# Reordering the opening of a two-layer kernel on one core: batch 1's choice first, batch 2's ranks ahead of the first tile, and products of ones in TensorE's waits

## The chip, the cores and the metric

The kernel runs on one core of one Trainium2 chip. The core has TensorE (PE, with its weight loads PEld), VectorE (DVE), ScalarE (ACT), GpSimd (POOL) and SyncE (SP), which work through five separate lists of instructions and wait for each other on semaphores only. The metric is the device time of one execution in microseconds, the median of several.

## The reference

The input x has 8 batches of 512 rows of 128 numbers. Two residual layers are computed in float32:

```python
x = x + _layernorm(_L0_attn_ref(_layernorm(x, axis=-1), W_in, b_in, W_out, b_out, decay, mix), axis=-1)
x = x + _layernorm(_L0_ffn_ref(_layernorm(x, axis=-1), gate_kernel, w0, w1, wo), axis=-1)
```

The first layer mixes each row with the row before it (`mix * x + (1 - mix) * shifted`), multiplies by `W_in`, adds a bias, takes relu, runs a decaying sum down the sequence (`state = state * decay + h_t`) and multiplies by `W_out`. The second is a mixture of experts: each row is multiplied by a gate of 8 columns, the two largest logits choose two of 8 experts, and each chosen expert computes

```python
layer_1 = _gmm(sorted_hidden, w0, onehot)
layer_2 = _gmm(sorted_hidden, w1, onehot)
intermediate = jax.nn.silu(layer_1) * layer_2
layer_3 = _gmm(intermediate, wo, onehot)
```

with inner width 512. The two results of a row are summed with softmax weights.

## The kernel before, in words

**Two halves.** The 4096 rows make 8192 pairs of row and expert. The first layer goes batch by batch (512 rows each, four blocks of 128). The second goes tile by tile: 71 tiles of 128 pairs that belong to one expert. Between the two lies a table in DRAM, `expert_rows`, with a region for each expert. After a batch is chosen, its rows are written there by 8 indirect DMAs that GpSimd issues (`send_row`, L394). A tile is read back by one plain DMA that SyncE issues (`load_tile`, L312).

**What a batch does, in order.** `start1` and `offset1` (DVE) give the first norm, `normalise1` (ACT) applies it, `turn1` (PE, L1298) turns the four blocks, `shift` (ACT) and `mix_rows` (DVE, L757) mix the rows, `times_w_in` (PE, L1306) multiplies, `relu` (ACT), `scan` (DVE, L765) is the decaying sum, `times_w_out` (PE, L1313 and L1317) multiplies again. `start2` and `residual` (DVE, L771, L780) norm the result and add it to x. `start3`, `offset3` (DVE), `normalise3` (ACT, L524), `turn2` (PE, L1326), `turned` (ACT, L531) and `times_gate` (PE, L1333) lead to the gate's logits. `top` and `choose` (DVE, L812 to L839) pick the two experts. `ranks` (PE, L1340 to L1349) counts how many earlier rows went to each expert, and `put` (DVE, L846 to L866) makes the places in the table from it. `send_row` waits for those places. From batch 2 on, the roots of the second norm are taken by GpSimd (`late_power`, L382 and L385).

**The table of tiles.** `full_tiles` to `use_tiles` (DVE, L880 to L938) find out which expert and which rows each of the next 8 tiles has. Phase 1 (tiles 0 to 7) needs batches 0 and 1. SyncE waits for that table and then for all rows of both batches to have landed (L325) before it loads tile 0.

**Weights.** w0 and w1 are each split in two parts. ACT rounds a piece (`round_w`, L537, 8 pieces). The remainders are subtracted by GpSimd for w0 and by DVE for w1 (`split_rest`, L256, 8 half pieces).

**Order.** Each engine's list is written out by hand: an opening, and then a loop over slots, one tile to a slot, in which pieces of the later batches (`a_slot`) are interleaved with the tiles. In slot t PE turns tile t (L1376), multiplies tile t-1 by w0 and w1 (L1381 to L1383, six products), turns back tile t-2 (L1416) and multiplies tile t-3 by wo (L1432). `x_hi` (ACT, L570) and `x_lo` (DVE, L1099) split a turned tile before it is multiplied. In slot 1 PE turns batch 4 (`turn1(4)`, L1298), for which batch 3's `residual` must be done, because both use one bank of PSUM. In the kernel before, DVE's `put(2)` and PE's `ranks(2)` and `times_w_out(3)` stand in slot 0, behind tile 0.

## Time and profile before

| what | value |
|---|---|
| median of 3 runs | 347.58 us (345.55 to 349.6) |
| the profiled execution | 350.95 us, span 349.2 us |
| mean granted clock of TensorE | 0.858 |
| busy: PE, PEld | 262.5 us (75%), 220.8 us (63%) |
| busy: DVE, ACT, POOL | 199.7 us (57%), 179.4 us (51%), 180.1 us (52%) |
| first tile on PE | 64.72 us |
| last matmul | before 320 us |

Busy time is an average over three stages that have different limits: the opening up to the first tile at 64.72 us, the tiles, and the last norm after some 320 us. The granted clock is the share of full speed (2.4 GHz) that TensorE had; 0.50 is 1.2 GHz. The span is the time between the first and the last record of the profiled execution, and its own time is 1.75 us longer.

### The profile page before, as it was taken

Reading aid. Unit: us, or ns where it says so; the run is one execution under the profiler, and the core shown is the slowest. Engines: PE = TensorE matmul, PEld = TensorE weight load, DVE = VectorE, ACT = ScalarE, POOL = GpSimd, SP = SyncE. Lnnn points to the kernel's source line nnn. Section 1 sums busy time; section 2 is a strip of 40 time slices with the busy share of each in tenths; the row PEclk is TensorE's granted clock in tenths of the full one; section 3 lists DMA queues with packets and bytes.
Section 4 is the critical chain, followed back from the end, with each engine's and each line's share of the span. In section 5 each row is a group of like instructions: output and inputs, shape, how many; then the busy total and the mean of one; then the engine's idle time right before and its main releaser. Section 6 shows DMA issues by size and latency. Waiting matters only on the chain.

```text
span 349.2 us, 6768 instructions
## 1 busy us (share of the span) xinstructions
PE 262.5 (75%) x1615; PEld 220.8 (63%) x1615; DVE 199.7 (57%) x896; ACT 179.4 (51%) x436; POOL 180.1 (52%) x199
## 2 busy tenths in 40 slices
PE   1645515579997999699969969969999999995000
PEld 0323513468785888588858858848888888885000
DVE  4787969564662495348347625633334455459763
ACT  3475635345654566354545544524655565554362
POOL 6065567155465656545754764465333333335673
PEclk9975555589999899789989998998999999999555
DMA  6999111211221131013112211331233100190225
GB/s 160 225 362 281 41 38 55 52 33 41 60 57 46 41 76 48 30 52 81 41 35 64 57 47 42 83 92 55 69 85 79 42 23 23 31 401 29 90 60 150
DMA packets 27971, 29.48 MB, mean 84 GB/s; under 512 B 4538, under 2 KB 21148, under 8 KB 27936
## 3 DMA queue, kind: packets, MB, share of 16 engines
q1 hardware_dynamic: 22672, 20.00, 20.2%
q0 software_dynamic: 4544, 8.93, 8.0%
q8 instruction: 16, 0.26, 0.3%
q10 hardware_dynamic: 720, 0.13, 0.2%
q14 instruction: 19, 0.16, 0.2%
HBM read 17.49 MB, written 12.01 MB: 84 GB/s over the span
## 4 chain that ended last, share of the span: by engine, by line
PE 60%; DVE 15%; ACT 8%; another core or an unknown queue 6%; POOL 4%; issue 4%; DMA 2%; SPq 0%; ACTq 0%; DVEq 0%; POOLq 0%
PE bank L1432 14%; PE bank L1381 9%; PE bank L1383 9%; PE bank L1382 8%; PE bank L1416 8%; PE bank L1376 3%; POOL expert_rows L394 2%; PE bank L1317 2%; PE bank L1333 2%; ACT sb_w_raw L593 2%; DVE sb_rs L1171 2%; PE bank L1326 2%; ACT sb_row L524 1%; PE bank L1306 1%
## 5 line engine op out<-in xcount | busy, mean ns | idle before, releaser
L405 POOL DMA_INDIRECT pair_rows<-sb_y_rows,sb_y_pair x71 | 70.4, 991 | 99.3 <-ACT sb_y_rows L587 75.2
L394 POOL DMA_INDIRECT expert_rows<-sb_row,sb_place x64 | 65.1, 1016 | 32.0 <-issue 18.0
L1106 DVE TENSOR_TENSOR sb_w_raw<-bank,sb_w_raw 128x512 f32<-128x512 f32 x71 | 49.0, 690 | 51.9 <-PE bank L1383 33.7
L1432 PE MATMUL bank<-sb_w_raw,sb_gatedT 128*128 x568 | 76.4, 279 | 0.0
L1432 PEld LDWEIGHTS bank<-sb_w_raw,sb_gatedT 128*128 128x128 f32 x568 | 70.6, 196 | 0.1
L1381 PE MATMUL bank<-sb_w_parts,sb_x_hi 128*128 x142 | 65.2, 459 | 3.5 <-ACT sb_w_raw L575 1.9
L580 ACT ACTIVATE sb_gatedT<-bank 128x512 f32<-128x512 f32 x71 | 42.5, 599 | 45.3 <-PE bank L1416 32.0
L1099 DVE TENSOR_TENSOR sb_x_lo<-bank,sb_x_hi 128x128 fp32r<-128x128 f32 x71 | 20.4, 288 | 66.9 <-ACT sb_x_hi L570 60.6
L1383 PE MATMUL bank<-sb_w_parts,sb_x_hi 128*128 x142 | 58.5, 412 | 0.0
L1382 PE MATMUL bank<-sb_w_parts,sb_x_lo 128*128 x142 | 58.1, 409 | 0.0
L575 ACT ACTIVATE sb_w_raw<-bank 128x512 f32<-128x512 f32 x71 | 42.7, 601 | 18.4 <-PE bank L1383 14.3
L570 ACT ACTIVATE sb_x_hi<-bank 128x128 fp32r<-128x128 f32 x71 | 19.7, 277 | 58.2 <-PE bank L1376 35.7
L1416 PE MATMUL bank<-sb_ident,sb_w_raw 128*128 128x128 f32 x284 | 44.2, 280 | 0.4 <-issue 0.4
L1416 PEld LDWEIGHTS bank<-sb_ident,sb_w_raw 128*128 128x128 f32 x284 | 35.5, 144 | 9.9 <-issue 2.6
L1381 PEld LDWEIGHTS bank<-sb_w_parts,sb_x_hi 128*128 128x128 f32 x142 | 28.2, 199 | 10.3 <-issue 6.9
L1383 PEld LDWEIGHTS bank<-sb_w_parts,sb_x_hi 128*128 128x128 f32 x142 | 28.1, 198 | 7.0
L1382 PEld LDWEIGHTS bank<-sb_w_parts,sb_x_lo 128*128 128x128 f32 x142 | 28.4, 200 | 3.2
L1376 PE MATMUL bank<-sb_ident,sb_taken_rows 128*128 128x128 f32 x71 | 20.4, 287 | 4.6 <-DMA sb_taken_rows<-expert_rows 4.0
L587 ACT ACTIVATE sb_y_rows<-bank 128x128 f32<-128x128 f32 x71 | 19.5, 274 | 1.0 <-PE bank L1432 0.9
L1306 PE MATMUL bank<-sb_early,sb_w_inT 128*128 128x512 f32 x16 | 11.4, 803 | 10.2 <-DVE sb_early L757 10.2
L1326 PE MATMUL bank<-sb_ident,sb_row 128*128 128x128 f32 x32 | 7.5, 378 | 14.4 <-ACT sb_row L524 14.3
L256 POOL TENSOR_TENSOR sb_w_parts<-sb_w_raw,sb_w_parts 128x512 fp32r<-128x512 f32 x8 | 9.9, 1271 | 15.4 <-ACT sb_w_parts L537 15.4
(162 smaller groups left out, 353.4 us busy)
## 6 DMA issues: line engine op xcount, KB each, us to landing
sb_taken_rows<-expert_rows SPq DMA_DIRECT2D x71, 65.0 KB
sb_w_raw<-in_L_ffn_w SPq DMA_DIRECT2D x2, 2048.0 KB, 15.1
sb_w_raw<-pair_rows SPq DMA_DIRECT2D x2, 1024.0 KB, 7.8
out_dram<-sb_x SPq DMA_DIRECT2D x3, 512.0 KB, 3.2
pair_rows<-sb_y_rows,sb_y_pair POOLq DMA_INDIRECT x71
sb_x<-in_L_attn_x SPq DMA_DIRECT2D x4, 256.0 KB, 5.5
expert_rows<-sb_row,sb_place POOLq DMA_INDIRECT x64
sb_w_raw<-pair_rows SPq DMA_DIRECT2D x2, 512.0 KB, 3.4
```

The source lines that it names most:

```text
L394: pool.indirect_dma_start(expert_rows[:, :], bass.IndirectOffsetOnAxis(ap=place[b % ROWS][:, k, j:j + 1], axis=0), row[b % ROWS][:, j, :], ...
L405: pool.indirect_dma_start(pair_rows[:, :], bass.IndirectOffsetOnAxis(ap=y_pair[group % 2][:, t % PAIRS:t % PAIRS + 1], axis=0), y_rows[slo ...
L575: act.activation(silu[t % 2][:], p_l1[:], ACT.Silu).then_inc(c["silu"], 1)
L580: act.activation(gatedT[t % 2][:], p_gatedT[:], ACT.Copy).then_inc(c["gatedT"], 1)
L1099: dve.tensor_tensor(x_lo[t % 2][:], p_xeT[:, 0:P], x_hi[t % 2][:].bitcast(F32), ALU.subtract).then_inc(c["x_lo"], 1)
L1106: dve.tensor_tensor(gated[t % 2][:], p_l2[:], silu[t % 2][:], ALU.mult).then_inc(c["gated"], 1)
L1376: pe.transpose(p_xeT[:, 0:P], taken_rows[:, t % RING, 0:D], ident[:]).then_inc(c["xeT_ps"], 1)
L1381: pe.matmul(to, x_hi, w_hi, start=True, stop=False)
L1382: pe.matmul(to, x_lo, w_hi, start=False, stop=False)
L1383: return pe.matmul(to, x_hi, w_lo, start=False, stop=True)
L1416: last = pe.transpose(p_gatedT[:, n * P:(n + 1) * P], gated[t % 2][:, n * P:(n + 1) * P], ident[:])
L1432: last = pe.matmul(p_y[t % 2][:, 0:D], gatedT[t % 2][:, n * P:(n + 1) * P], wo.rearrange("p o d -> p (o d)"), start=(n == 0), stop=(n == F ...
```

## The change

It touches the opening of four engines and slot 0 of the loop.

- DVE: `offset1(3)`, `top(1)`, `choose(1)` and `put(1)` move ahead of `rest_mean_var` and `start2(2)`. `put(2)` moves out of slot 0, in front of the loop. Five of the eight half pieces of `split_rest` come last. The last steps of the table of phase 1 stand behind `top(2)` and `choose(2)`.
- ACT: `round_w(4)` and `round_w(5)` move ahead of `normalise3(1)`; `relu(3)` ahead of `root(3, 2)`; `rest_root` and `turned(2)` change places with others.
- PE: `times_gate(1)` moves ahead of `times_w_out(2)`; `ranks(2)` and `times_w_out(3)` move out of slot 0, in front of tile 0. A new function `fill(n)` issues n products of ones with ones, 128x128 by 128x512 in bf16, into the bank `p_l1` that nothing else uses before tile 0. There are 60 such products in 12 places.

```diff
@@ ACT, opening
             root(3, 1, mv3, sd3)
+            round_w(4)
+            round_w(5)
             normalise3(1, 0, G)
-            round_w(4)
             turned(1)
             root(1, 3, mv1, sd1)
-            round_w(5)
-            rest_root()
+            round_w(6)
+            normalise1(3, 0, G)
+            round_w(7)
+            shift(3)
             root(2, 2, mv2, sd2)
-            round_w(6)
-            round_w(7)
-            normalise1(3, 0, G)
-            shift(3)
+            relu(3)
             root(3, 2, mv3, sd3)
             normalise3(2, 0, G)
+            rest_root()
+            turned(2)
             act.activation(unused[:], eps[:], ACT.Silu)
-            relu(3)
-            turned(2)
             normalise1(4, 0, G)
@@ DVE, slot 0 and opening
                 if s == 0 and part == 0:
-                    if k == 0:
-                        put(2)
                     if table:
                         full_tiles(p)
...
             rest_sums(8, 16)
-            rest_mean_var()
-            start2(2)
+            offset1(3)
             top(1)
             choose(1)
-            offset1(3)
             put(1)
+            start2(2)
+            mix_rows(3)
+            residual(2)
+            start3(2)
             split_rest(0, 1)
-            residual(2)
+            offset3(2)
+            rest_mean_var()
             split_rest(1, 3)
-            start3(2)
-            mix_rows(3)
-            split_rest(3, 4)
-            offset3(2)
+            scan(3)
+            rest_offset()
             full_tiles(1)
             expert_ends(1)
             experts_past(1)
             experts_of_tiles(1)
+            top(2)
+            choose(2)
             rows_skipped(1)
             rows_of_tiles(1)
             use_tiles(1)
-            split_rest(4, 6)
-            scan(3)
-            split_rest(6, 8)
-            rest_offset()
-            top(2)
-            choose(2)
+            put(2)
+            split_rest(3, 8)
@@ PE
+            def fill(n):
+
+                for _ in range(n):
+                    pe.matmul(p_l1[:], ones_b[:],
+                              ones_b[:, None, :].broadcast_to([P, G, P]), start=True, stop=True)
...
                 if part == 0:
-                    if k == 0 and s == 0:
-                        ranks(2)
-                        times_w_out(3)
...
             times_w_in(1)
+            fill(2)
             turn1(2)
+            fill(3)
             times_w_out(1)
+            fill(10)
             times_w_in(2)
             turn2(0)
+            fill(2)
             times_gate(0)
+            fill(7)
             ranks(0)
+            fill(5)
             turn2(1)
+            fill(2)
+            times_gate(1)
             times_w_out(2)
-            times_gate(1)
+            fill(1)
             ranks(1)
             turn1(3)
+            fill(6)
             times_w_in(3)
+            fill(8)
             turn2(2)
+            fill(2)
             times_gate(2)
+            times_w_out(3)
+            ranks(2)
+            fill(12)
```

VectorE from batch 3's first norm to batch 1's choice, before (`sb_rest_mv` belongs to the norms of batches 4 to 7, L771 to `start2(2)`, L812 to L819 to `top(1)`):

```order
L737 BN_STATS sb_rest_stats<-sb_x 128x6 x8
L744 BN_AGGR sb_rest_mv<-sb_rest_stats 128x2 x16
L771 BN_STATS sb_stats_0<-bank 128x6 x4
L707 BN_AGGR sb_mv_0<-sb_stats_0 128x2 x4
L812 MAX sb_top_1<-bank 128x8 x4
L816 MAX_INDEX sb_choice_1<-sb_top_1,bank 128x8 x4
```

and the same place in the changed kernel (L714 and L720 are `offset1(3)`):

```order
L737 BN_STATS sb_rest_stats<-sb_x 128x6 x8
L714 RECIPROCAL sb_rs_1<-sb_sd_1 128x4
L720 SCALAR_TENSOR_TENSOR sb_nm_1<-sb_mv_1,sb_rs_1 128x4
L812 MAX sb_top_1<-bank 128x8 x4
L816 MAX_INDEX sb_choice_1<-sb_top_1,bank 128x8 x4
```

Two groups of norms no longer stand in front of the choice.

VectorE at the end of the opening, in the changed kernel, from the last step of `choose(2)` over the table (L917 to L938) and `put(2)` (L846 to L866) to tile 0's `x_lo` (L1097 there):

```order
L839 TENSOR_REDUCE sb_taken<-sb_taken 128x8
L917 TENSOR_REDUCE sb_skipped<-sb_past_skip 128x8
L919 TENSOR_SCALAR sb_tile_chunk_i<-sb_tile_expert 128x8
L926 SCALAR_TENSOR_TENSOR sb_tile_row_i<-sb_tile_f,sb_used,sb_skipped 128x8
L932 TENSOR_SCALAR sb_clipped<-sb_ends 128x9
L935 TENSOR_TENSOR sb_take<-sb_clipped 128x8
L938 TENSOR_TENSOR sb_used<-sb_used,sb_take 128x8
L846 TENSOR_TENSOR sb_rank_f<-bank,sb_region_f 128x32
L856 TENSOR_SCALAR sb_count_i<-bank 128x8
L861 TENSOR_TENSOR sb_place_0<-sb_onehot,sb_rank_f 128x32 x2
L866 TENSOR_REDUCE sb_place<-sb_place_0 128x8
L256 TENSOR_TENSOR sb_w_parts<-sb_w_raw,sb_w_parts 128x4x128 x5
```

Before, tile 0's `x_lo` stood directly behind L839; the four rows L846 to L866 followed it, and the table and the five half pieces had been done earlier.

TensorE around tile 0 (the first L1376), before:

```order
L1326 MATMUL bank<-sb_ident,sb_row 128x128 x4
L1333 MATMUL bank<-sb_gate,sb_early 128x8 x4
L1376 MATMUL bank<-sb_ident,sb_taken_rows 128x128
L1340 MATMUL bank<-sb_taken,sb_ones_b 128x8
L1342 MATMUL bank<-sb_taken,sb_before_b 128x32
L1346 MATMUL bank<-sb_taken,sb_ones_b 128x24
L1346 MATMUL bank<-sb_taken,sb_ones_b 128x16
L1346 MATMUL bank<-sb_taken,sb_ones_b 128x8
L1349 MATMUL bank<-sb_taken,sb_ones_b 128x32
L1313 MATMUL bank<-sb_b_parts,sb_ones_b 128x512
L1317 MATMUL bank<-sb_w_outT,sb_early 128x128 x4
```

and in the changed kernel (L1294 are the products of ones, L1316 and L1320 `times_w_out(3)`, L1343 to L1352 `ranks(2)`):

```order
L1294 MATMUL bank<-sb_ones_b 128x512 x2
L1336 MATMUL bank<-sb_gate,sb_early 128x8 x4
L1316 MATMUL bank<-sb_b_parts,sb_ones_b 128x512
L1320 MATMUL bank<-sb_w_outT,sb_early 128x128 x4
L1343 MATMUL bank<-sb_taken,sb_ones_b 128x8
L1345 MATMUL bank<-sb_taken,sb_before_b 128x32
L1349 MATMUL bank<-sb_taken,sb_ones_b 128x24
L1349 MATMUL bank<-sb_taken,sb_ones_b 128x16
L1349 MATMUL bank<-sb_taken,sb_ones_b 128x8
L1352 MATMUL bank<-sb_taken,sb_ones_b 128x32
L1294 MATMUL bank<-sb_ones_b 128x512 x12
L1376 MATMUL bank<-sb_ident,sb_taken_rows 128x128
```

Batch 2's ranks and batch 3's product now stand in front of tile 0, and twelve products of ones between them and it.

## Rows read from the trace of the kernel before

**Rows 1.** Windows: busy us (instructions) per engine, TensorE's granted clock, DMA share, GB/s
```profile
core 0: us, PE busy (x) PEld busy (x) DVE busy (x) ACT busy (x) POOL busy (x), PEclk, DMA share, GB/s
20.00:25.00 5.00, 2.02 (x9) 1.70 (x9) 4.82 (x17) 3.50 (x5) 4.05 (x4) 0.66 1.05 376
...
60.00:65.00 5.00, 0.99 (x6) 0.83 (x6) 2.96 (x22) 1.65 (x4) 0.39 (x1) 0.50 0.11 27
```

**Rows 2.** Chain of waits, 59 to 86 us: start us, us, what
```profile
59.43 2.29 DMA expert_rows<-sb_row,sb_place
...
65.35 0.42 PE bank L1313
...
72.51 0.23 PE bank L1381
...
76.09 0.34 PE bank L1381
...
78.03 0.89 PE bank L1432 x8
...
84.89 0.23 PE bank L1313
```

**Rows 3.** Timeline, POOL: start us, us, engine, line, op [idle before it and its releaser]
```profile
36.96 1.09 POOL L394 DMA_INDIRECT expert_rows<-sb_row,sb_place  x1 [4.60 <-DVE sb_place L866]
...
49.38 0.96 POOL L394 DMA_INDIRECT expert_rows<-sb_row,sb_place  x1 [2.47 <-DVE sb_place L866]
50.65 1.88 POOL L394 DMA_INDIRECT expert_rows<-sb_row,sb_place  x1 [0.30 <-issue]
```

**Rows 4.** Timeline, DVE, opening
```profile
32.71 0.39 DVE L812 MAX8 sb_top<-bank 128x8 f32<-128x8 f32 x4 [1.24 <-PE bank L1333]
...
35.83 0.22 DVE L866 TENSOR_REDUCE sb_place<-sb_place 128x8 int32<-128x64 f32 x1
...
44.80 0.17 DVE L825 CAST sb_choice_f<-sb_choice 128x8 f32<-128x8 uint32 x1 [1.15 <-DVE sb_choice L816]
45.51 0.23 DVE L828 TENSOR_TENSOR sb_onehot<-sb_expert_f,sb_choice_f 128x64 bf16<-128x64 f32 x1 [0.54 <-DVE sb_choice_f L825]
...
48.35 0.22 DVE L866 TENSOR_REDUCE sb_place<-sb_place 128x8 int32<-128x64 f32 x1 [1.14 <-DVE sb_place L861]
...
50.40 1.29 DVE L256 TENSOR_TENSOR sb_w_parts<-sb_w_raw,sb_w_parts 128x512 fp32r<-128x512 f32 x2
...
57.01 1.29 DVE L256 TENSOR_TENSOR sb_w_parts<-sb_w_raw,sb_w_parts 128x512 fp32r<-128x512 f32 x2
...
62.98 0.22 DVE L839 TENSOR_REDUCE sb_taken<-sb_taken 128x8 bf16<-128x40 bf16 x1
65.53 0.29 DVE L1099 TENSOR_TENSOR sb_x_lo<-bank,sb_x_hi 128x128 fp32r<-128x128 f32 x1 [2.33 <-ACT sb_x_hi L570]
65.74 0.18 DVE L846 TENSOR_TENSOR sb_rank_f<-bank,sb_region_f 128x32 f32<-128x32 f32 x1
...
66.42 0.16 DVE L880 TENSOR_SCALAR sb_tiles_i<-sb_count_i 128x8 int32<-128x8 int32 x1
...
67.63 0.89 DVE L771 BATCH_NORM_STATS2 sb_stats<-bank 128x6 f32<-128x128 f32 x4 [0.64 <-PE bank L1317]
```

**Rows 5.** Timeline, PE, opening
```profile
26.77 2.07 PE L1306 MATMUL bank<-sb_early,sb_w_inT 128*128 128x512 f32 x2 [3.53 <-DVE sb_early L757]
...
30.69 1.87 PE L1333 MATMUL bank<-sb_gate,sb_early 128*128 128x8 f32 x8 [0.69 <-ACT sb_early L531]
34.90 0.19 PE L1340 MATMUL bank<-sb_taken,sb_ones_b 128*128 128x8 bf16 x1 [2.34 <-DVE sb_taken L839]
...
64.72 0.47 PE L1376 MATMUL bank<-sb_ident,sb_taken_rows 128*128 128x128 f32 x1 [4.01 <-DMA sb_taken_rows<-expert_rows]
...
71.77 0.63 PE L1298 MATMUL bank<-sb_ident,sb_early 128*128 128x128 f32 x4 [1.87 <-DVE sb_x L780]
```

**Rows 6.** Timeline, ACT: `normalise3(1)`
```profile
35.16 1.65 ACT L524 ACTIVATE sb_row<-sb_x,sb_nm,sb_rs 128x128 f32<-128x128 f32 x4 [3.66 <-DVE sb_nm L720]
```

## The prediction

> **What bounds the opening now.** I read the page first, then the windows, the chain of waits, and the timelines of POOL, DVE and PE up to 72 us. The windows show TensorE losing its clock between 20 and 25 us (granted 0.66), and at half speed, 1.2 GHz, in the last one before the tiles, with 0.99 us of work in 5 [rows 1]. That alone costs nothing where PE waits for others. The chain says who it waits for: the last row send of batch 1 is issued at 59.43 us and landed 2.29 us later [rows 2], and tile 0 is turned at 64.72 us, 3.0 us behind that landing, after 4.01 us of idle time [rows 5]. GpSimd issues the sixteen sends from 36.96 us. Batch 0's end at 46.91 us (49.38 less the idle 2.47), and then GpSimd sits until batch 1's places come [rows 3]. So the opening is bounded by GpSimd's sixteen sends and by VectorE, which delivers both sets of places.
>
> VectorE is nearly as tight. From the end of `put(0)` at 36.05 us to the end of `choose(2)` at 63.20 us lie 27.15 us of its list, of which 2.83 us are three waits for its own results (1.15, 0.54, 1.14 us) in batch 1's choice and places, the stretch under batch 0's sends and just behind them [rows 4]. Then it idles 2.33 us until tile 0 is turned.
>
> Behind tile 0 the point to watch is `turn1(4)` at 71.77 us, before which PE idles 1.87 us for batch 3's residual [rows 5]. It hangs on `sums2(3)`, which DVE starts at 67.63 us after 0.64 us of idle time for `times_w_out(3)` [rows 4]. From there to `turn1(4)` are 4.14 us through DVE and POOL that the change does not touch.
>
> **The change, part by part.**
>
> *Ones before `ranks(0)`.* In front of `top(0)` DVE idles 1.24 us for the gate's products, which take 1.87 us at half clock [rows 4, 5]. If the ones hold the clock, nearly all of that idle time goes; I leave 0.09 us, so **1.15 us** are won, and `put(0)` ends at 34.9 us, the first send starts at 35.8 us. The bounds: 1.24 us, and a loss if the ones are late themselves (rival D). The price of one product of ones is that of the nearest row, the bias product over 512 columns in bf16: 0.23 us in a dense stream at full clock, 0.42 us at half [rows 2]. Ten take 2.3 us in a gap of 3.53, seven 1.6 us in a gap of 2.34 [rows 5]; at full clock they cost nothing.
>
> *Batch 1's choice first.* `put(1)` now comes right after batch 3's first norm, some 8 us after `put(0)`, stalls included, so at about 43 to 45 us, before batch 0's sends are out (35.8 + 9.95 = 45.75). GpSimd's wait of 2.47 us goes. The last send starts at 35.8 + 9.95 + 0.30 + 10.05 = 56.1 us (batch 0's eight, a gap, batch 1's from first to last start [rows 3, 2]), has landed at 58.4 us, and tile 0 can be turned at 61.4 us, `x_lo(0)` 0.81 us later at 62.2 us. By the sends alone the gain there is 65.53 - 62.2 = 3.3 us.
>
> *VectorE's sum.* Its list up to `x_lo(0)` holds the same work as before and `put(2)`, 0.68 us (65.74 to 66.42) [rows 4]: 34.9 + 27.15 + 0.68 = **62.7 us**, if it stalls as often as before. That is 0.5 us later than the sends allow, so DVE sets the time. The table of phase 1 comes before five half pieces (5 x 0.645 = 3.2 us, from the pairs of 1.29), `put(2)` and some 0.45 us, at 58.4 us, together with the landing. The five half pieces used to stand before a wait of 2.33 us, where a late DVE cost nothing; now they stand on the path.
>
> *Slot 0.* Before, `sums2(3)` began 2.10 us after `x_lo(0)` (65.53 to 67.63): `put(2)` 0.68 and 0.64 of waiting are now gone, and 0.78 us remain. So `sums2(3)` starts at 62.7 + 0.8 = 63.5 us, **4.1 us** earlier than 67.63, and `turn1(4)` at 67.7 us.
>
> *ACT.* `round_w(4)` and `(5)` move into the 3.66 us that it waited in front of `normalise3(1)` [rows 6] and take about 2 us there: nothing. If that cover were gone, `normalise3(1)` would be late by as much, but batch 1's gate has slack until DVE asks for it some 4 us later.
>
> *The last twelve ones.* They follow `ranks(2)`, at about 58 us by the sums above, and end near 61 us at full clock, just in front of tile 0: nothing. At half clock they end at 63.1 us and hold tile 0 back by 1.7 us, `x_lo(0)` by 1.2 us.
>
> *After `turn1(4)`.* Before, tile 1's products there ran partly at half clock: 3.58 us from its first product (72.51) to tile 2's (76.09), less 0.21 for a turn, where tile 2's took 1.94 us (76.09 to 78.03) [rows 2]. Up to 1.4 us lie in that. But PE will idle there again for batch 3's residual, some 2.5 us, longer than the 1.87 us of before, so I take nothing and keep 1.4 us as the bound above; below, a clock lower still for one more tile costs 1.4 us.
>
> *The tiles.* After 72 us PE is the engine that is busy throughout, and its list, like those of the others, is unchanged. The sends of batch 2 are interleaved with the tiles and move with them. A shift of the start is a shift of the end.
>
> The sum is 4.1 us. The profiled execution took 350.95 us, so it would take 346.9. It lies 3.4 us above the median of the three runs, which themselves spread over 4 us; against the median of 347.58 us the forecast is **343.5 us**.
>
> **A rule against this change.** One send took 1.88 us instead of 0.96 [rows 3]; it started at 50.65 us, while DVE subtracted half pieces, with two inputs from SBUF (50.40, 1.29 us) [rows 4]. The stalls of DVE's small steps came in the stretch of the sends as well. In the changed kernel sends run without a break from 35.8 to 57 us, and batch 2's choice moves into their last part. I give this as rival C, from the rows, and its extreme as E. The Trainium skill, GPSIMD Engine Reference, section 1 (Specifications), says that GpSimd shares its SBUF interfaces with VectorE and contends with instructions that have two SBUF inputs or run in a two-port mode. By that rule the stretched send and the stalls are one thing, and more overlap means more of both.
>
> **The rivals.**
>
> A. The forecast: as many stalls as before, clock held. Chance 0.50, its own range 341.8 to 345.5 us.
>
> B. *More.* The stalls do not recur, and a send isn't stretched (0.9 us less). Then the sends bound: `x_lo(0)` at 61.3, `sums2(3)` at 62.1, a gain of 5.5 us; with the full clock after `turn1(4)` 6.9. Time 340.7 to 342.1 us. For it: `choose(2)` and the table ran before almost without a stall. Against it: batch 1's choice lies under sends as it did. Chance 0.15.
>
> C. *GpSimd's sends stall batch 2's choice too.* Another 2.83 us in DVE's list, which has no slack left: a gain of 1.3 us, 346.3 us. Chance 0.18.
>
> D. *The ones don't hold the clock.* Then they cost 0.42 us each and stand ahead of work that is waited for. Ten take 4.2 us from 23.24 to 27.4, where 26.77 was the start of the next product; seven more end at 36.2 us, where `ranks(0)` started at 34.90. Everything is 2.45 us later than in A, and the last twelve end at 65.6 us: `x_lo(0)` 66.4, `sums2(3)` 67.2, a gain of 0.4 us, 347.2 us. Against it: two stretches of ones are the densest work that PE gets there. Chance 0.09.
>
> E. *Slower.* The same mechanism as C, at DVE's end of the opening: batch 1's choice, batch 2's choice, the table's fourteen dependent steps and `put(2)` with the half pieces each stall 2.83 us under sends. Each stall counts in full, since the 2.33 us of idle time in front of `x_lo(0)` are gone: 4 x 2.83 - 2.83 = 8.5 us against 4.1, so 352.0 us. It decides from 6.9 us of stalls on, and is slower by 1% from 10.4. For it: three stalls came in one batch. Against it: the table's steps ran before under batch 1's sends almost freely, between 54 and 57 us. Chance 0.08.
>
> **How the numbers follow.** A difference of 1%, 3.5 us, is about what a measurement of this kernel can tell from none. The forecast lies only 0.6 us beyond it. B and three quarters of A are faster by more, 0.52; a quarter of A, C and D are within, 0.40; E is slower, 0.08. The range of 340.5 to 347.5 us takes in A, B, C and D, and leaves out E and the outer ends.
>
> **What would show it.** Right: granted clock near 1 between 25 and 60 us, DVE without the wait in front of `top(0)`, sixteen sends of GpSimd with no wait longer than 0.5 us between them, tile 0 turned at about 61.5 us, and `turn1(4)` at about 67.7 us. C or E: waits of DVE for its own results in `choose(2)` or the table, and `x_lo(0)` at 65 us or later with tile 0 turned before. D: granted clock 0.50 and ones ending after the work behind them was ready. The forecast would be wrong in kind if the tiles behind 72 us do not keep the distance that the opening won.

## The result, and the profile after

The changed kernel takes 352.8 us (median of 4 runs, 351.38 to 353.7). The kernel before, beside it, takes 348.09 us (4 runs, 345.55 to 349.6). The ratio is 1.0134, 95% interval [1.0085, 1.0184]: **slower by 1.3%**, where 343.5 us and a gain of 4.1 us were forecast. The profiled execution of the changed kernel took 352.79 us (span 351.1, granted clock 0.904), that of the kernel before 350.95 us. Some executions of a kernel take over 1.5% longer than its fastest (the profiled one of the kernel before, 350.95 against 345.55 us, is such a one), and every ratio in this document leaves these out, so that a ratio and two medians may differ.

The sends come first, since they were the aim. GpSimd's own list is the same in both kernels; what moves its sends is when their places come. GpSimd's timeline of the changed kernel (start, duration, instruction, [idle time before it and its releaser]):

```profile
37.47 1.09 POOL L394 DMA_INDIRECT expert_rows<-sb_row,sb_place  x1 [5.08 <-DVE sb_place L866]
...
47.75 0.96 POOL L394 DMA_INDIRECT expert_rows<-sb_row,sb_place  x1 [0.30 <-issue]
...
56.60 0.96 POOL L394 DMA_INDIRECT expert_rows<-sb_row,sb_place  x1 [0.30 <-issue]
70.11 1.22 POOL L394 DMA_INDIRECT expert_rows<-sb_row,sb_place  x1 [12.54 <-DVE sb_place L866]
```

They did what the change was to do: sixteen sends with 0.30 us between them, the last one starting at 56.60 us instead of near 59 [rows 2]. Tile 0 no longer waits for them. It waits for TensorE, whose timeline is:

```profile
30.72 1.87 PE L1336 MATMUL bank<-sb_gate,sb_early 128*128 128x8 f32 x8
32.45 3.15 PE L1294 MATMUL bank<-sb_ones_b 128*128 128x512 bf16 x7
...
43.38 0.64 PE L1301 MATMUL bank<-sb_ident,sb_early 128*128 128x128 f32 x4
43.85 1.46 PE L1294 MATMUL bank<-sb_ones_b 128*128 128x512 bf16 x6
48.99 2.08 PE L1309 MATMUL bank<-sb_early,sb_w_inT 128*128 128x512 f32 x2 [3.69 <-DVE sb_early L757]
50.86 3.62 PE L1294 MATMUL bank<-sb_ones_b 128*128 128x512 bf16 x8
61.79 1.11 PE L1329 MATMUL bank<-sb_ident,sb_row 128*128 128x128 f32 x4 [7.30 <-ACT sb_row L524]
...
67.98 3.16 PE L1294 MATMUL bank<-sb_ones_b 128*128 128x512 bf16 x12
70.97 0.31 PE L1376 MATMUL bank<-sb_ident,sb_taken_rows 128*128 128x128 f32 x1
...
77.08 0.63 PE L1301 MATMUL bank<-sb_ident,sb_early 128*128 128x128 f32 x4 [2.67 <-DVE sb_x L780]
```

Tile 0 (L1376) is turned at 70.97 us, 6.25 us later than before [rows 5]. In front of it PE stood idle for 7.30 us before `turn2(2)` (L1329), waiting for ACT's `normalise3(2)`. ACT's timeline shows why that was late:

```profile
47.47 0.69 ACT L508 ACTIVATE sb_early<-bank,sb_one_minus_mix 128x511 f32<-128x511 f32 x1 [4.05 <-remote]
...
58.77 0.69 ACT L513 ACTIVATE sb_early<-bank,sb_b_in 128x512 f32<-128x512 f32 x1 [10.43 <-issue]
...
60.09 1.65 ACT L524 ACTIVATE sb_row<-sb_x,sb_nm,sb_rs 128x128 f32<-128x128 f32 x4 [0.34 <-issue]
...
71.32 0.28 ACT L570 ACTIVATE sb_x_hi<-bank 128x128 fp32r<-128x128 f32 x1 [4.73 <-PE bank L1376]
```

These two waits are the finding of the case. `shift(3)` (L508) reads what PE's `turn1(3)` wrote. PE's record of that ends at 43.38 + 0.64 = 44.02 us, but ACT starts at 47.47. `relu(3)` (L513) reads the product that ended at 48.99 + 2.08 = 51.07 us, but ACT starts at 58.77, 7.7 us later, having done nothing for 10.43. PE has only the eight ones left to do, and they end at 50.86 + 3.62 = 54.48 us, 4.3 us before `relu(3)` starts. By the records no engine is at work on anything that ACT needs. Nor is ACT short of instructions: the queues that carry them move nothing between 43.5 and 78 us of this trace. The profile names no releaser. "Remote" means that an update of the awaited semaphore is recorded just before the start, but long after the recorded end of the work; "issue" means that no such update is found in the records. The chain of waits (start, duration, what) has the same two pieces:

```profile
42.48 0.95 ACT sb_w_parts L537
43.42 4.03 another core or an unknown queue
47.45 0.02 issue
47.47 0.69 ACT sb_early L508
48.16 0.18 ACT sb_sd L481
48.34 10.43 issue
58.77 0.69 ACT sb_early L513
```

I call such a stretch a **late signal**: the work waited for is recorded as done, the waiting engine is free, and it starts microseconds later. It is a name for what is seen, not yet a cause: the profile models the ends of PE's products, so a product may also have ended later than its record says. For `shift(3)` the update of the semaphore is on record at 47.45 us, 3.4 us behind that end. The Trainium skill, Perfetto Trace Analysis, section Per-engine timelines, draws the propagation of a semaphore update as a stage of its own behind an instruction's recorded end. That agrees with what is seen, but the page gives it no such length, and 7.7 us is this trace's number.

VectorE's timeline shows the consequence:

```profile
32.75 0.39 DVE L812 MAX8 sb_top<-bank 128x8 f32<-128x8 f32 x4 [1.23 <-PE bank L1336]
...
35.79 0.19 DVE L846 TENSOR_TENSOR sb_rank_f<-bank,sb_region_f 128x32 f32<-128x32 f32 x1 [0.64 <-PE bank L1352]
...
44.62 0.19 DVE L846 TENSOR_TENSOR sb_rank_f<-bank,sb_region_f 128x32 f32<-128x32 f32 x1 [1.47 <-PE bank L1352]
...
48.19 0.75 DVE L757 SCALAR_TENSOR_TENSOR sb_early<-bank,sb_mix,sb_early 128x512 f32<-128x512 f32 x1 [1.47 <-ACT sb_early L508]
...
59.68 0.18 DVE L714 RECIPROCAL sb_rs<-sb_sd 128x4 f32<-128x4 f32 x1 [7.37 <-ACT sb_sd L481]
...
65.61 0.39 DVE L812 MAX8 sb_top<-bank 128x8 f32<-128x8 f32 x4 [0.47 <-PE bank L1336]
...
72.22 0.28 DVE L1097 TENSOR_TENSOR sb_x_lo<-bank,sb_x_hi 128x128 fp32r<-128x128 f32 x1
...
72.94 0.89 DVE L771 BATCH_NORM_STATS2 sb_stats<-bank 128x6 f32<-128x128 f32 x4
```

`offset3(2)` (L714) needs a root that stands on ACT behind `relu(3)`, and 7.37 us pass. Behind it stand batch 2's choice, the table of tiles 0 to 7 and `put(2)`.

Last the windows (engines' busy time, then granted clock, DMA share, GB/s):

```profile
20.00:25.00 5.00, 4.86 (x26) 2.81 (x24) 4.82 (x17) 3.49 (x5) 4.04 (x4) 0.90 1.06 377
25.00:30.00 5.00, 2.20 (x7) 1.29 (x8) 4.56 (x26) 3.15 (x8) 3.50 (x4) 0.79 1.05 289
30.00:35.00 5.00, 5.00 (x18) 2.62 (x16) 3.52 (x28) 3.35 (x6) 2.40 (x2) 0.50 1.01 279
...
55.00:60.00 5.00, 0.00 (x0) 0.00 (x0) 0.29 (x3) 0.97 (x3) 1.95 (x3) 0.84 0.12 40
```

The ones raised the clock before 30 us, from 0.66 in the window from 20 to 25 us [rows 1] to 0.90, and lost it where it was wanted: 0.50 from 30 to 35 us, with `times_gate(0)` and `ranks(0)` in it. From 55 to 60 us PE does nothing at all.

### The profile page after: what moved, and what is told of

It reads as the page before. It is cut to its first block, busy times and chain, and to the rows that moved or that the text cites. A ratio compares the mean times of both kernels' runs of the same rounds, so it can differ in the third digit from the quotient of the medians.

```text
span 351.1 us, 6888 instructions
## 1 busy us (share of the span) xinstructions
PE 272.6 (78%) x1675; PEld 219.7 (63%) x1675; DVE 199.1 (57%) x896; ACT 178.6 (51%) x436; POOL 180.0 (51%) x199
## 4 chain that ended last, share of the span: by engine, by line
PE 55%; DVE 12%; ACT 11%; issue 8%; another core or an unknown queue 7%; POOL 4%; DMA 2%; SPq 0%; ACTq 0%; DVEq 0%; POOLq 0%
PE bank L1432 13%; PE bank L1383 8%; PE bank L1381 8%; PE bank L1382 8%; PE bank L1416 7%; ACT sb_row L524 2%; PE bank L1336 2%; PE bank L1376 2%; PE bank L1294 2%; PE bank L1329 2%; ACT sb_w_raw L593 2%; DVE sb_rs L1169 2%; ACT sb_early L498 1%; PE bank L1320 1%
## 5 line engine op out<-in xcount | busy, mean ns | idle before, releaser
L394 POOL DMA_INDIRECT expert_rows<-sb_row,sb_place x64 | 64.8, 1013 | 36.0 <-issue 18.3
L1432 PE MATMUL bank<-sb_w_raw,sb_gatedT 128*128 x568 | 75.0, 275 | 0.0
L1432 PEld LDWEIGHTS bank<-sb_w_raw,sb_gatedT 128*128 128x128 f32 x568 | 69.0, 192 | 0.1
L1381 PE MATMUL bank<-sb_w_parts,sb_x_hi 128*128 x142 | 63.8, 449 | 1.5 <-DVE sb_w_raw L1104 0.6
L1097 DVE TENSOR_TENSOR sb_x_lo<-bank,sb_x_hi 128x128 fp32r<-128x128 f32 x71 | 20.5, 288 | 66.6 <-ACT sb_x_hi L570 52.2
L1383 PE MATMUL bank<-sb_w_parts,sb_x_hi 128*128 x142 | 56.8, 400 | 0.0
L1382 PE MATMUL bank<-sb_w_parts,sb_x_lo 128*128 x142 | 56.5, 398 | 0.0
L1416 PE MATMUL bank<-sb_ident,sb_w_raw 128*128 128x128 f32 x284 | 43.0, 274 | 0.7 <-issue 0.7
L1416 PEld LDWEIGHTS bank<-sb_ident,sb_w_raw 128*128 128x128 f32 x284 | 34.4, 141 | 10.5 <-issue 3.4
L1381 PEld LDWEIGHTS bank<-sb_w_parts,sb_x_hi 128*128 128x128 f32 x142 | 27.5, 194 | 8.8 <-issue 5.8
L1383 PEld LDWEIGHTS bank<-sb_w_parts,sb_x_hi 128*128 128x128 f32 x142 | 27.1, 191 | 6.6
L1382 PEld LDWEIGHTS bank<-sb_w_parts,sb_x_lo 128*128 128x128 f32 x142 | 27.5, 194 | 3.0
L1376 PE MATMUL bank<-sb_ident,sb_taken_rows 128*128 128x128 f32 x71 | 20.1, 282 | 4.7 <-DVE sb_x_lo L1097 2.6
L1329 PE MATMUL bank<-sb_ident,sb_row 128*128 128x128 f32 x32 | 7.2, 366 | 18.7 <-ACT sb_row L524 16.6
L1294 PE MATMUL bank<-sb_ones_b 128*128 128x512 bf16 x60 | 21.2, 501 | 0.0
L1329 PEld LDWEIGHTS bank<-sb_ident,sb_row 128*128 128x128 f32 x32 | 4.9, 187 | 21.9 <-ACT sb_row L524 19.1
```

Of the source, the lines that this page charges most:

```text
L394: pool.indirect_dma_start(expert_rows[:, :], bass.IndirectOffsetOnAxis(ap=place[b % ROWS][:, k, j:j + 1], axis=0), row[b % ROWS][:, j, :], ...
L1294: pe.matmul(p_l1[:], ones_b[:], ones_b[:, None, :].broadcast_to([P, G, P]), start=True, stop=True)
L1376: pe.transpose(p_xeT[:, 0:P], taken_rows[:, t % RING, 0:D], ident[:]).then_inc(c["xeT_ps"], 1)
L1381: pe.matmul(to, x_hi, w_hi, start=True, stop=False)
L1382: pe.matmul(to, x_lo, w_hi, start=False, stop=False)
L1383: return pe.matmul(to, x_hi, w_lo, start=False, stop=True)
```

## The experiments

Theory **S**: signals between engines come late while GpSimd's row sends follow one another without a pause, and the change puts the chain `shift(3)`, `relu(3)`, root, `normalise3(2)` under sixteen such sends. Rival **O**: the products of ones hold the signals up. Each set of runs has its own runs of the kernel before (B below).

**Without the ones; the ones alone; without batch 3's ones.**

```diff
 e1_no_ones: the changed kernel, fill(n) does nothing
-                for _ in range(n):
-                    pe.matmul(p_l1[:], ones_b[:],
...
+                return
 e2_ones_alone: the kernel before, with fill(n) and its 60 products in the same 12 places
 e3_no_ones_batch3: the changed kernel without
-            fill(6)
             times_w_in(3)
-            fill(8)
```

> The changed kernel without its 60 products of ones; the rest of its order is kept. In the changed kernel relu(3) on ScalarE waits 10.43 us (to 58.77 us) although the product it waits for is recorded as ended at 51.07, and shift(3) waits 4.05 us (to 47.47) although its turn ended at 44.02. Theory S (signals): signals between the engines arrive late while GpSimd's sixteen row sends are in flight without a break; both waits are released with the last landing of a batch's sends. Then they stay here: relu(3) starts 5 us or more behind the end of times_w_in(3), tile 0 is turned at about 71 us, the time is that of the changed kernel within 1.5 us. Theory O (ones): products of ones queued behind a product hold its signal back. Then both waits are gone, tile 0 is turned at 62 to 65 us, and the time is 345 to 349 us.

> The kernel before with the 60 products of ones in its own order, the other parts of the change left out. Theory S: GpSimd's sends keep their gap between the batches and start later against the work, so relu(3) is not held; the time is that of the kernel before within 1% and tile 0 is turned within 1 us of 64.7. Theory O: relu(3) starts 5 us or more behind the end of times_w_in(3), and the time is 3 us or more above that of the kernel before.

> The changed kernel without the 6 and the 8 products of ones around times_w_in(3); the other 46 stay. Theory O: shift(3) and relu(3) follow their products within 0.5 us, tile 0 is turned before 66 us. Theory S: relu(3) waits until the last of batch 1's sends has landed (near 58.6 us), tile 0 is turned near 71 us.

Measured, B 352.9 us: without the ones 357.14 us, 1.0126 [1.0022, 1.023]; the ones alone 354.3 us, 1.005 [1.0014, 1.0087]; without batch 3's ones 357.5 us in one run. Both theories miss at one of the two waits. Without any ones `shift(3)` starts at 48.42 us, 4.2 us behind the recorded end of its turn, against O. But `relu(3)` starts at 52.06 us, where its product is recorded from 49.95 to 52.03 us: it follows at once, as O said and against S, which wanted 5 us or more. Without batch 3's ones it is the same (`shift(3)` at 49.00 us, `relu(3)` at 52.64, 0.04 us behind its product). The loss stays all the same: tile 0's `x_hi` starts at 70.33 and 72.73 us, where O wanted tile 0 turned by 65 and 66. **O falls as the cause of the loss**, but the long wait at `relu(3)` itself appears only where ones stand behind its product. What took the time instead is on VectorE and is shown below, behind the table of the five sets. The ones are no gain either: alone they cost 0.5%, with tile 0 turned at 65.81 us.

**The second eight sends held until `relu(3)` is written.**

```diff
 e4_sends_wait_relu3 and g2_sends_wait_again: the changed kernel, GpSimd
             for b in (0, 1):
+                if b == 1:
+                    pool.wait_ge(a["hidden"], 4)
                 for n in range(K * G):
                     send_row(b, n)
```

> The changed kernel, but GpSimd begins batch 1's sends only when relu(3) is done. Theory S: with a pause in the sends the signal of times_w_in(3) arrives when batch 0's last send has landed, at 49 to 52 us; the sends end near 62, tile 0 is turned near 66 us, some 4 us below the changed kernel. Theory O: relu(3) still waits some 7 us behind its product, to 58 us, the sends start then and end at 69, tile 0 is turned near 73 us or later.

> The changed kernel, GpSimd's second eight sends held until relu(3) has been written (the one look gave 352.5 us against 352.9 for the kernel before). S: with late signals it is within 0.5% of the kernel before and 1% faster than the changed kernel, tile 0's x_hi at 66 to 67 us; without late signals it is no faster than the changed kernel, since the wait only delays the sends. Rival (the order is longer in itself): it ends with the changed kernel or behind it in every set.

The first execution (e4) took 352.49 us against B 352.9, with `relu(3)` at 49.03 and tile 0 turned at 66.27 us, as S had it. Ten executions (g2) gave 347.69 us, B 349.48, ratio 1.0039 [0.9958, 1.012], while the changed kernel in the same set took 355.71 us, 1.0274 [1.0088, 1.0459]. The rows of the held kernel, GpSimd, ACT and PE:

```profile
50.33 0.96 POOL L394 DMA_INDIRECT expert_rows<-sb_row,sb_place  x1 [2.97 <-issue]
```

```profile
44.50 0.69 ACT L510 ACTIVATE sb_early<-bank,sb_one_minus_mix 128x511 f32<-128x511 f32 x1 [1.18 <-PE bank L1303]
...
48.84 0.69 ACT L515 ACTIVATE sb_early<-bank,sb_b_in 128x512 f32<-128x512 f32 x1 [2.65 <-PE bank L1311]
```

```profile
65.36 0.33 PE L1378 MATMUL bank<-sb_ident,sb_taken_rows 128*128 128x128 f32 x1 [3.38 <-DMA sb_taken_rows<-expert_rows]
```

and ACT of the changed kernel in the same set:

```profile
53.16 0.69 ACT L513 ACTIVATE sb_early<-bank,sb_b_in 128x512 f32<-128x512 f32 x1 [7.03 <-remote]
```

A pause of 2.97 us in GpSimd's row starts `relu(3)` 4.3 us earlier and turns tile 0 at 65.36 instead of 70.66 us. A wait was added and the kernel got 8 us faster than the changed one; 5.3 us of them are there when tile 0 is turned. That is the clearest support for S, in the wider sense that engines are held up while the sends run without a pause. PE now waits for the rows again, and the gain over the kernel before is gone with the pause.

**Pausing for the landings, one send in flight, the kernel before again, short rows.**

```diff
 e7_pause_landed: the changed kernel, GpSimd, ahead of batch 1's eight sends
+                if b == 1:
+                    pool.wait_ge(s_sent[0], sent_by(0))
 e6_one_in_flight: ahead of each of batch 1's sends
+                    if b == 1:
+                        pool.wait_ge(s_sent[0 if n == 0 else 1], 16 * (K * G if n == 0 else n))
 e5_short_rows and g4_short_rows_again: 32 columns of each row instead of 130
-                    row[b % ROWS][:, j, :], None).then_inc(s_sent[b % ROWS], 16)
+                    row[b % ROWS][:, j, D - 30:], None).then_inc(s_sent[b % ROWS], 16)
...
```

> The kernel before once more with a profile, to see how far its opening repeats. Theory S expects what its first trace had: tile 0 turned within 1 us of 64.7 us, waits of ScalarE or VectorE for late signals in the opening below 4 us in all, because its sends pause between the batches. If instead tile 0 moves by more than 3 us from one execution to the next, the loss of the changed kernel is scatter of the opening.

> The changed kernel, ones included, with one wait added: GpSimd begins batch 1's sends only when all of batch 0's have landed, a pause of some 1.5 us. Theory S (signals pile up while sends follow each other without a break): the long waits shrink as with the pause for relu(3) (tile 0 at 66.3 us there); tile 0 is turned at 64 to 67 us and the time is below that of the changed kernel by 3 us or more, within 1% of the kernel before. If only the number of sends in flight matters and not the break, relu(3) stays late by more than 5 us and the time is that of the changed kernel plus 1.5 us.

> The changed kernel, but each of batch 1's eight sends waits until the one before has landed, so a send takes some 2.2 us instead of 1.26. Batch 1's sends then end near 66 us and tile 0 is turned near 70 us, whatever the theory. What tells: under theory S, signals in that stretch are prompt, relu(3) and root(3, 2) on ScalarE wait less than 0.5 us beyond what they wait for, and normalise3(2) is done before 54 us. If signals are late there too, one send in flight is enough to hold them.

> The changed kernel, but a send writes 32 columns of each row (128 bytes) instead of 130 (520 bytes); the number of sends, rows and their places stay. The tiles compute on a constant in the other columns. If the bytes of the sends hold the signals back, relu(3) follows times_w_in(3) within 1 us and tile 0 is turned before 66 us. If it is GpSimd's issuing, or the number of rows, the waits stay: shift(3) and relu(3) wait 4 us or more in all for signals, tile 0 is turned at 69 us or later.

This set ran on another chip, and **there the kernel before takes 324.76 us** (13 runs, 323.03 to 326.14), 28 us less than in the set before. The short rows take 322.67 us, the pause for the landings 324.36 (ratio 0.9987 [0.9953, 1.0021]), one send in flight 333.21. In none of the four traces is a late signal: in the three of the changed kernel `relu(3)` waits at most 2.71 us, and for PE. So none of the three edits tested S here. The kernel before has tile 0 turned at 62.03 us instead of 64.72, more than the 1 us that was allowed for. Only the price of one send in flight is plain: tile 0 is turned at 74.97 us, after a wait of 14.62 us for its rows.

What the set does tell is in the kernel before itself. One row groups all 71 `x_hi` (busy, mean ns | idle before, by releaser), first in the trace that the prediction read, then in this set:

```profile
L570 ACT ACTIVATE sb_x_hi<-bank 128x128 fp32r<-128x128 f32 x71 | 19.7, 277 | 58.2 <-PE bank L1376 35.7 <-remote 20.8 <-issue 1.6
```

```profile
L570 ACT ACTIVATE sb_x_hi<-bank 128x128 fp32r<-128x128 f32 x71 | 19.7, 277 | 46.2 <-PE bank L1376 46.1
```

The 20.8 us of "remote" are six waits, and in the second trace there is none. The first of them, at tile 12:

```profile
112.19 0.28 ACT L570 ACTIVATE sb_x_hi<-bank 128x128 fp32r<-128x128 f32 x1 [4.44 <-remote]
```

PE had turned that tile at 107.90 us. From the first `x_hi` to the last the first trace takes 246.2 us (65.22 to 311.45), the second one 223.9 (62.55 to 286.45). The two rows don't explain all of the 22.3 us between them: the second has no "remote", but 10.4 us more of waiting for PE, so `x_hi` as a whole waits 58.2 instead of 46.2 us, 12.0 us more. The other 10 us are not traced. In both traces GpSimd's sends follow each other some 1.3 us apart while it has any. A gapless row of sends is thus not enough for a late signal.

Something else separates the two kinds of trace, and it is a **rival that was not tested**. The kernel's instructions update semaphores 1526 times. Counted in the traces, 0 to 2 of these updates have no record in the four of this set, and 158 to 195 have none in each of the sixteen others. Every execution on record was made while its instructions and signals were being recorded. If the recording holds the engines up where it loses records, then the late signals, and the 28 us between the chips, may be its doing and not the kernel's or the chip's. No execution without recording tells.

**The changed kernel again and again, with and without ones; batch 2's work ahead of tile 0 alone; short rows again.**

```diff
 f1_batch2_ahead_alone and g3_batch2_ahead_again: the kernel before, DVE and PE
-                    if k == 0:
-                        put(2)
...
+            put(2)
...
-                    if k == 0 and s == 0:
-                        ranks(2)
-                        times_w_out(3)
...
+            times_w_out(3)
+            ranks(2)
 f0, g1, h1, h2: the changed kernel; f2: as e1; f3: the kernel before
```

> The changed kernel as it is, timed and traced once more. The kernel before took 348, 353 and 325 us in three sets of runs, and in the last of them no signal between engines was late in the traces. So the question is what the change is worth with and without late signals. Theory S: where the traces of this set show none (kernel before near 325 us), shift(3) and relu(3) follow their products within 0.5 us, tile 0 is turned at about 61.5 us as forecast, against 62.4 in the kernel before, and the changed kernel is 2 to 5 us faster. Where they show them (kernel before near 350 us), relu(3) is late by 3 us or more and the changed kernel is 2 to 6 us slower. Rival: the change loses 3 us or more in either case, because of its order.

> The changed kernel without its 60 products of ones, in the same set. If the ones are worth what the idle time in front of top(0) and the half clock on the first tiles promise, it is 1 to 3 us slower than the changed kernel. If the clock is worth nothing here, the two are equal within 0.7 us.

> The kernel before with one part of the change: put(2) on VectorE in front of the loop, ranks(2) and times_w_out(3) on TensorE in front of tile 0. No ones, and batch 1's choice and the sends where they were. Slot 0 becomes shorter by put(2) and the wait for times_w_out(3), 1.3 us before batch 3's sums. With or without late signals it is 0.5 to 1.5 us faster than the kernel before, since the idle time of 2.3 us in front of tile 0 covers what is moved there.

> The kernel before, for its trace in this set. Near 325 us: no wait for late signals beyond 1 us in the loop, tile 0 turned at 62 to 63 us. Near 350 us: ScalarE waits 3 to 4.5 us at tile 12, 20, 28 and 36 for a turn that is recorded as long done, tile 0 turned at 64 to 66 us.

> The changed kernel a third time, timed beside the kernel before. Theory S (signals between engines come late while GpSimd's sixteen sends run without a pause): if this set's traces show such waits (ACT's shift(3) or relu(3) idle for 3 us or more), tile 0's x_hi starts 5 us or more later than in the kernel before and the time is 0.9 to 1.4% longer. If the set shows none (the kernel before takes about 325 us), tile 0's x_hi starts at or before 62.8 us and the kernel is faster than before, by up to 1.2% (the 4.1 us forecast). Rival (the moved order is itself longer, whatever the signals): slower by 0.9 to 1.4% in either kind of set.

> The kernel before with put(2), ranks(2) and times_w_out(3) ahead of the first tile, and nothing else. It measured 0.9949 of the kernel before. If that is real it is again 0.3 to 0.7% faster, with the slots after tile 0 closer together; if it was chance, within 0.3% on either side. S says nothing against it: batch 1's sends still wait for batch 1's places.

> The changed kernel with 32 columns (128 bytes) of each row sent and fetched instead of 130 columns; the tiles compute on a constant in the other columns. The same number of sends and of rows. If bytes in flight make the signals late: in a set in which the changed kernel shows waits of 3 us or more at shift(3) or relu(3), this one shows none over 1.5 us. If it is the number of rows or sends: the same waits as the changed kernel. In a set without late signals it tells nothing.

> The changed kernel a fourth time beside the kernel before. The three earlier sets of runs in which the kernel before took 348 to 353 us were on two other chips than the set in which it took 325 us, where no late signals were seen. Theory S: on a chip without late signals (before about 325 us) tile 0's x_hi starts by 62.8 us, where the kernel before had it at 62.76 us, and the time is 0 to 1.2% shorter; on a chip with them (before about 350 us) the time is 0.9 to 2.7% longer, with a wait of 3 us or more at shift(3) or relu(3) and tile 0's x_hi at 70 us or later. Rival (the moved order is itself longer): slower on either.

> The changed kernel a fifth time beside the kernel before, for the case not yet seen, a chip with prompt signals. Theory S: there (before about 325 us) tile 0's x_hi starts by 62.8 us and the time is 0 to 1.2% shorter; on a chip with late signals (before about 350 us) it is 0.9 to 2.7% longer. Rival (the moved order is itself longer): slower on either.

The changed kernel in five sets, the last four on four different chips (waits in us, by the profile):

| set | B, us | ratio | wait at `shift(3)`, `relu(3)` | tile 0's `x_hi`, us |
|---|---|---|---|---|
| after | 348.09 | 1.0134 [1.0085, 1.0184] | 4.05, 10.43 | 71.32 |
| f0 | 352.96 | 1.0093 [1.0022, 1.0164] | 6.27, 9.76 | 72.33 |
| g1 | 349.48 | 1.0274 [1.0088, 1.0459] | 1.18, 7.03 | 70.97 |
| h1 | 353.82 | 1.0091 [1.005, 1.0132] | 2.02, 7.52 | 71.65 |
| h2 | 350.41 | 1.0119 [1.0028, 1.021] | 1.21, 6.08 | 71.16 |

The loss is real in all five. Its place is not only ACT's waits. In g1 and h2 `shift(3)` follows its turn by 0.1 us and `relu(3)` starts at 53.16 and 52.55 us, some 6 us earlier than in the first trace, and yet tile 0 is no earlier. VectorE's rows of g1 tell why (L744 is `rest_mean_var`):

```profile
54.36 0.70 DVE L744 BATCH_NORM_AGGREGATE sb_rest_mv<-sb_rest_stats 128x2 f32<-128x6 f32 x9
55.93 0.25 DVE L744 BATCH_NORM_AGGREGATE sb_rest_mv<-sb_rest_stats 128x2 f32<-128x6 f32 x2 [0.87 <-issue]
57.36 0.18 DVE L744 BATCH_NORM_AGGREGATE sb_rest_mv<-sb_rest_stats 128x2 f32<-128x6 f32 x1 [1.18 <-issue]
58.76 0.25 DVE L744 BATCH_NORM_AGGREGATE sb_rest_mv<-sb_rest_stats 128x2 f32<-128x6 f32 x2 [1.22 <-issue]
60.16 0.25 DVE L744 BATCH_NORM_AGGREGATE sb_rest_mv<-sb_rest_stats 128x2 f32<-128x6 f32 x2 [1.15 <-issue]
```

These sixteen instructions wait for one signal, before the first of them, and for nothing after it:

```python
                dve.wait_ge(rest["stats"], 1)
                for n in range((B - REST) * G):
                    last = dve.bn_aggr(rest_mv[:, n, :], rest_stats[:, n, :])
```

Still VectorE stands idle for 4.42 us between them, 4.03 us in h2, and 1.7 to 4.6 us in e1, e3, f2 and g4. A signal that travels late can't explain an idle time in front of an instruction that waits for none. Whatever it is, it holds an engine up and not only a signal. What the traces have in common is the sum: VectorE's idle time between the end of `put(0)` and `x_lo(0)`, without its last wait, for `x_hi` (pieces of 0.15 us or more):

| kernel (traces) | VectorE idle, us |
|---|---|
| changed kernel (after, f0, g1, h1, h2) | 10.8, 12.5, 9.3, 11.2, 9.2 |
| without ones (e1, f2), without batch 3's ones (e3), short rows (g4) | 10.0, 9.5, 9.7, 9.5 |
| batch 1's sends held for `relu(3)` (e4, g2) | 3.4, 0.9 |
| kernel before (its first trace, f3), ones alone (e2), batch 2's work alone (f1, g3) | 3.0, 4.2, 3.5, 4.7, 3.7 |
| the chip of 325 us: kernel before (e0), the three edits (e5, e6, e7) | 0.2, 0.4, 0.4, 0.4 |

None of these sets fell on the chip where the kernel before takes 325 us, so the case that both theories wanted, the changed kernel beside the kernel before with prompt signals, **was not measured**.

Without ones (f2) 356.71 us, 1.0159 [1.0062, 1.0255], overlapping f0's, so neither of the two values that were expected is decided. In its ACT rows `shift(3)` is late as with them, by 4.2 us, and `relu(3)` is not: its product is recorded as ended at 49.94 + 2.08 = 52.02 us.

```profile
48.41 0.69 ACT L508 ACTIVATE sb_early<-bank,sb_one_minus_mix 128x511 f32<-128x511 f32 x1 [5.48 <-remote]
52.05 0.69 ACT L513 ACTIVATE sb_early<-bank,sb_b_in 128x512 f32<-128x512 f32 x1 [2.77 <-issue]
```

**Batch 2's work ahead of tile 0 alone** measured 350.8 us, 0.9949 [0.99, 0.9998], then 348.97 us, 1.0133 [0.9891, 1.0376]. The first interval ends just below 1 and the second holds it: no effect is established. The kernel before in f0's set (f3) took 355.07 us in one run, tile 0's `x_hi` at 65.35, as before.

**Short rows again** leave out most of each row: the tiles compute on a constant in 96 of the columns. Where the kernel took 322.67 us before, it now took 354.78 (one run each), with B at 349.48, and ACT waited as in the changed kernel beside it:

```profile
53.45 0.69 ACT L517 ACTIVATE sb_early<-bank,sb_b_in 128x512 f32<-128x512 f32 x1 [7.04 <-remote]
```

7.04 us with 128 bytes in a row, 7.03 with 520 (4.4 us behind the recorded end of the product in both). In the one pair of traces, **the bytes in flight are not what makes it late**; the number of rows and sends, which this edit leaves, or the sends' cadence may be.

## Why the prediction was wrong, step by step

**Batch 1's choice first: right on the sends.** `put(1)` was in time, the gap of 2.47 us is gone, the last send starts at 56.60 us (forecast 56.1). The rest of the step, tile 0 turned at 61.4, assumed that only rows and VectorE hold tile 0. On the fast chip even the kernel before has no such gap (start, duration, [idle]; GpSimd, batch 0's last send and batch 1's first):

```profile
45.98 1.31 POOL L394 DMA_INDIRECT expert_rows<-sb_row,sb_place  x1 [0.30 <-DVE sb_place L866]
47.59 0.96 POOL L394 DMA_INDIRECT expert_rows<-sb_row,sb_place  x1 [0.30 <-issue]
```

The gap that I set out to see closed [rows 3] came from VectorE's 2.83 us of stalls [rows 4], which are absent there. It was a symptom of whatever holds the engines up, and the change removed the symptom by running the sends closer together.

**VectorE's sum: the step that failed.** It said 62.7 us for `x_lo(0)`, "if it stalls as often as before". Measured 72.22. The work was sized right: from the end of `put(0)` at 36.57 to 72.22 are 35.65 us, less waits of 1.47, 1.47, 7.37 and 0.47 leaves 24.87, against 27.15 + 0.68 - 2.83 = 25.0 forecast. The waits are 10.8 us where 2.83 were assumed, 8.0 more, and `put(0)` ended 1.67 later than 34.9. That is the whole 9.5 us. The error behind it: I counted VectorE's own list and took the inputs from ACT and PE as in time, and the stalls as no longer than before when the sends lose their pause. In the first trace the chain through `relu(3)`, which now stands ahead of `root(3, 2)` and so of batch 2's root, carries most of it; in g1 and h2 half of it lies in `rest_mean_var`. No run moved `relu(3)` back, so the share of that one move is not shown. I had read three stalls of VectorE for its own results in that stretch [rows 4] and priced them as VectorE's trouble under contention; the traces after show idle time of the same kind on ACT too.

**Rival E** forecast 352.0 us and the measurement is 352.8, but that is luck of size: E wanted four stalls of 2.83 us in batch 1's choice, batch 2's choice, the table and `put(2)`, and there is one large one, on ACT, through a root. In g1 and h2 some 4 us are stalls within VectorE's list, which is nearer to E, but not at E's places: from `top(2)` on VectorE runs almost without a pause, since the sends are over by then. The rule that I cited for C and E, from the Trainium skill, GPSIMD Engine Reference, section 1 (Specifications), on interfaces that GpSimd and VectorE share, does not cover ACT's waits here, and no send of the changed kernel's sixteen was stretched (0.96 to 1.09 us each).

**Ones before `ranks(0)`: wrong in sign.** Forecast a gain of 1.15 us. `top(0)` still waits 1.23 us, seven ones took 3.15 us (0.45 each; rival D took 0.42 at half clock), `ranks(0)` came 0.49 us later, and the first send starts at 37.47 instead of 35.8 us. D's mechanism is right, its size too large, because the ten ones earlier did run at a higher clock. In one of the five profiles of this kernel (f0) they held it, and there the step came out as forecast, to 0.25 us. DVE no longer waits (no bracket), and the windows show the clock:

```profile
31.82 0.39 DVE L812 MAX8 sb_top<-bank 128x8 f32<-128x8 f32 x4
```

```profile
25.00:30.00 5.00, 1.94 (x8) 0.88 (x8) 4.56 (x25) 3.21 (x9) 3.66 (x3) 1.00 1.06 292
30.00:35.00 5.00, 3.84 (x27) 2.05 (x26) 4.54 (x37) 4.04 (x9) 2.50 (x2) 1.00 1.01 278
```

Its first send starts at 36.05 us, and the kernel is no faster for it: tile 0's `x_hi` at 72.33, the latest of the five.

**The last twelve ones** (nothing at full clock, up to 1.7 us at half) took 3.16 us, 0.26 each, and tile 0's product follows them directly at 70.97. Without ones tile 0 waited 3.0 us for its rows instead and `x_hi` started at 70.33 (e1) and 70.27 (f2, beside f0's 72.33): they cost 1 to 2 us at tile 0, which the whole times do not show.

**Slot 0 and "After `turn1(4)`": right.** `sums2(3)` starts 0.72 us after `x_lo(0)` (forecast 0.8), `turn1(4)` another 4.14 us later (forecast 4.1), after 2.67 us of PE's idle time (forecast some 2.5). **ACT's rounding cost nothing**, as said.

**The tiles: half right.** A shift of the start should be a shift of the end. `turn1(4)` moved from 71.77 [rows 5] to 77.08, 5.3 us, the last `x_hi` from 311.45 to 313.32, 1.9 us. In the one pair of profiles from a single set (f0 and f3) it is 5.6 us at `turn1(4)` and 2.7 at the last `x_hi`. Some 3 us come back along the tiles. About 0.9 of it is the clock right behind `turn1(4)`, which the range allowed for (the next two turned tiles are 2.52 us apart, 77.54 to 80.06, where they were 3.44, 72.23 to 75.67; granted clock 1.00 from 70 to 80 us, where the kernel before had 0.83). The rest stays open: in the first pair fewer late signals could explain it ("remote" before `x_hi` 18.3 instead of 20.8 us), in the second pair they are more (23.7 instead of 16.9) and it comes back all the same.

**What is shown and what is argued.** Shown: the loss arises between 43 and 61 us, as idle time of VectorE and ACT of some 9 to 12 us in VectorE's list (five sets); taking the ones away doesn't remove it (e1, f2, e3); a pause in the sends does (e4, g2). By one pair of traces: the bytes don't matter (g4). By one set: on one chip no such waits occur. Only where ones stand behind its product is `relu(3)` late, which neither theory explains. Argued: that a semaphore's update travels late; it can't be all, since VectorE also stalls where it waits for none. Open: what makes it so, the recording itself included, and whether the changed order would gain its 4.1 us on the chip without such waits. The nearest case, short rows on that chip, has tile 0's `x_hi` at 62.90 against 62.55, and `turn1(4)` at 68.08 against 69.08: little of 4.1 us, as the kernel before had no gap to close there.

## What to carry to other kernels

When a timeline shows an engine waiting for a result whose record ended microseconds earlier, and the releaser reads "remote" or "issue", expect such waits on every engine whose chain is moved into the same stretch, not only on the engine that showed them, and count an engine's idle time over the whole stretch: here it moved from one instruction to another between traces while its sum stayed at 9 to 12 us. Before closing a gap in a queue of DMA issues, ask what made the gap, and whether somebody's signals came through in it: here a pause of 3 us turned tile 0 5.3 us earlier. Time a kernel on more than one chip before trusting a difference of 1%, since here a whole class of waits was absent on one, and ask whether the recording takes part, since its gaps came and went with those waits.

## What the runs showed of the hardware that was not expected

- One and the same kernel took 324.76 us on one chip and 348 to 354 us in the sets on the others. From the first to the last tile the difference is 22.3 us, and the 71 waits of ACT's `x_hi` account for 12.0 of them (58.2 against 46.2 us).
- ACT started 7.7 us after the recorded end of the product that it waited for, under back-to-back sends by GpSimd of 0.96 us each (the first trace of the changed kernel). In another set it was 4.4 us, with rows of 128 and of 520 bytes alike.
- VectorE stood idle for 4.42 us between instructions that wait for nothing (g1), again under such sends.
- The traces with these waits lack the records of 158 to 195 of some 1526 semaphore updates, those without them of 0 to 2.
- Sixty products of ones do not settle the clock: the same kernel had granted clocks of 0.79 to 0.87 from 25 to 30 us and 0.50 from 30 to 35 in four profiles, and 1.00 in both in the fifth.
